# Graph attention, one core: the scaled accumulator enters TensorE's sum, and ScalarE writes it back

## The reference

```
q, k, v = x Wq + bq (scaled), x Wk + bk, x Wv + bv      # per node
s = sum over d of q[src] * k[dst]                        # per edge and head
attn = softmax of s over the edges with the same src
out[src] = sum of attn * v[dst];  y = layernorm(x + out Wo + bo)
```

## Time and profile before

| | us |
|---|---|
| three runs, median (lowest to highest) | 4021.01 (4016.24 to 4050.6) |
| the profiled execution: its time, its span | 4017.71, 4015.6 |
| busy: VectorE / GpSimd / TensorE / ScalarE | 3211.0 / 2447.6 / 2227.2 / 1504.6 |
| L931 gathers, 1794 of 1038 ns | 1863.0 busy, 583.7 idle before them |
| L790 and L797, 598 each, 952 and 946 ns | 569.2 and 565.5 |
| L844 and L836, 598 each, 429 and 426 ns | 256.6 and 255.0 |
| L1032 and L1034, 2392 and 1196 records | 902.0 and 497.3 |
| mean granted clock of TensorE | 0.743 of full speed |

### The profile page before, as it was taken

One profiled execution on the slowest core, in us unless ns is written; L12 is line 12 of the kernel. 1 busy time (PEld: TensorE's weight loads), 2 busy tenths in 40 slices (PEclk: granted clock), 3 DMA queues, 4 the chain that ended last, 5 costly groups with the idle time before them and its releaser, 6 DMA issues. The chain is left out here.

```text
span 4015.6 us, 59591 instructions
## 1 busy us (share of the span) xinstructions
PE 2227.2 (55%) x7109; PEld 1514.8 (38%) x7109; DVE 3211.0 (80%) x8164; ACT 1504.6 (37%) x6480; POOL 2447.6 (61%) x2365
## 2 busy tenths in 40 slices
PE   3999888653002555555555545555555555544776
PEld 3788775432001333333333333333333333323443
DVE  8554467799223999999999999999999999977776
ACT  0110002221001555555555555555555555534332
POOL 3221120003767777777777777777777777765677
PEclk9966568776555788778777787777877778766777
DMA  1211013226513788878887887888777788799222
GB/s 33 64 58 32 16 43 101 89 67 125 171 36 96 231 233 232 232 232 232 231 232 232 232 232 231 232 232 231 232 232 231 232 232 232 229 177 169 80 92 85
DMA packets 329217, 665.86 MB, mean 166 GB/s; under 512 B 63462, under 2 KB 191750, under 8 KB 329016
## 3 DMA queue, kind: packets, MB, share of 16 engines
q0 software_dynamic: 160768, 518.27, 46.4%
q1 hardware_dynamic: 168392, 146.96, 12.7%
HBM read 599.35 MB, written 65.86 MB: 166 GB/s over the span
## 5 line engine op out<-in xcount | busy, mean ns | idle before, releaser
L931 POOL DMA_INDIRECT kv<-kv_rows,idx x1794 | 1863.0, 1038 | 583.7 <-issue 538.5
L1032 PE MATMUL sum_ps<-pv,ident 128*128 128x264 f32 x2392 | 902.0, 512 | 1299.3 <-DVE pv L825 1299.3
L1032 PEld LDWEIGHTS sum_ps<-pv,ident 128*128 128x128 f32 x2392 | 511.3, 237 | 1712.1 <-DVE pv L825 1393.1
L987 ACT ACTIVATE pv<-kv,s 128x33 f32<-128x33 f32 x4784 | 1084.4, 309 | 53.9 <-ACT s L977 27.3
L790 DVE TENSOR_TENSOR prod<-kv,q 128x768 f32<-128x768 f32 x598 | 569.2, 952 | 59.7 <-DMA kv<-kv_rows,idx 59.6
L797 DVE TENSOR_REDUCE s<-prod 128x24 f32<-128x768 f32 x598 | 565.5, 946 | 0.0
L977 ACT ACTIVATE s<-s 128x32 f32<-128x32 f32 x598 | 137.0, 229 | 1126.1 <-DVE s L818 1126.1
L1034 PE MATMUL sum_ps<-pv,ident 128*128 128x264 f32 x1196 | 497.3, 508 | 0.0
L507 PE MATMUL hist_ps<-hot_lo,hot_hi 125*98 125x128 bf16 x1600 | 372.1, 409 | 121.7 <-DVE hot_hi L174 121.7
L825 DVE TENSOR_TENSOR pv<-kv,s 128x528 f32<-128x528 f32 x598 | 417.4, 698 | 0.3 <-ACT s L977 0.3
L507 PEld LDWEIGHTS hist_ps<-hot_lo,hot_hi 125*98 125x98 bf16 x1600 | 370.3, 259 | 123.2 <-issue 68.7
(11 more groups left out here) (164 smaller groups left out, 2450.5 us busy)
## 6 DMA issues: line engine op xcount, KB each, us to landing
q<-q_perm SPq DMA_DIRECT2D x598, 128.0 KB, 3.7
kv<-kv_rows,idx POOLq DMA_INDIRECT x1794, 4.0
kv_rows<-kv_st SPq DMA_DIRECT2D x98, 260.0 KB, 3.0
xt_sb<-in_xT SPq DMA_DIRECT2D x98, 128.0 KB, 3.2
node_rows<-q_st SPq DMA_DIRECT2D x98, 128.0 KB, 3.4
q_perm<-kv_st SPq DMA_DIRECT2D x98, 128.0 KB, 1.9
kv_st<-node_rows,node_id POOLq DMA_INDIRECT x98, 3.1
cols<-edge_keys,run_at POOLq DMA_INDIRECT x98, 2.5
```

The source lines that it names most:

```text
L931: pool.indirect_dma_start(out=kv[:, j, g, :], out_offset=None, in_=kv_rows, in_offset=bass.IndirectOffsetOnAxis(ap=idx[:, j, g:g + 1], axi ...
L987: last = act.activation(pv[:, b, V * VW + at_h:V * VW + at_h + HD + 1], kv[:, j, V, D + at_h:D + at_h + HD + 1], ACT.Copy, scale=s[:, b, V ...
L1032: pe.matmul(sum_ps[b][:, 0:VW], ident[:, :], pv[:, b, g * VW:(g + 1) * VW], start=g == 0, stop=False)
```

## The change

VectorE no longer adds the PSUM sum to the accumulator. It scales the accumulator of the step's tile into a fourth slot of `pv` (`carry`) and leaves `acc` as it is. TensorE takes that slot as a fourth product into the same bank, last. ScalarE then copies the finished bank into `acc` (`store`), with a table look-up of its own, in the middle of the next step's weighing: after three of the eight heads (BEFORE_STORE = 3). VectorE's `step` looks up first, now into two register sets rather than three, copies the old maximum right after the sum of products and before the weighing, and puts the carry between mask and maximum. ScalarE's copy of the indices moves from before the exponential to behind the weighing. The bound on the PSUM bank's reuse is now given by the order itself, so TensorE's wait for `acc_added` is gone, and its peeled steps with it. The table's scratch space moves from `pv` and `prod` into `kv`; `pv` grows by a slot.

```diff
@@ one_round @@
-        pv = sb("pv", [P, 2, G * VW])
-
-        room = pv[:, :, :].rearrange("p b w -> p (b w)")
...
+        pv = sb("pv", [P, 2, (G + 1) * VW])
+
+        room = kv[:, :, :, :].rearrange("p u g w -> p (u g w)")
...
@@ -797,9 +798,12 @@
                     dve.tensor_reduce(s[:, b, 0:G * HEADS], prod[:, :, :].rearrange("p g (h d) -> p (g h) d", d=HD),
                                       AX.X, ALU.add).then_inc(scored, 1)
 
-                def mask_scores(k, b, col, tile):
+                def old_maximum(k, b, tile):
 
                     dve.tensor_copy(s[:, b, G * HEADS:], runmax[:, bass.ds(tile * HEADS, HEADS)]).then_inc(old_copied, 1)
+
+                def mask_scores(k, b, col):
+
                     dve.wait_ge(scored, k + 1)
                     sv = s[:, b, 0:G * HEADS].rearrange("p (g h) -> p g h", h=HEADS)
                     dve.tensor_tensor(sv, sv, mflat[:, bass.ds(col, G)].unsqueeze(2).to_broadcast([P, G, HEADS]), ALU.add).then_inc(masked, 1)
@@ -827,50 +831,37 @@
                                       s[:, b, 0:V * HEADS].rearrange("p (g h) -> p g h", h=HEADS).unsqueeze(3).to_broadcast([P, V, HEADS, HD + 1]),
                                       ALU.mult).then_inc(pv_made, 1)
 
-                def scale_acc(k, b, tile, first=False):
-
+                def carry(k, b, tile, first=False):
                     if not first:
-                        dve.wait_ge(acc_added, k)
-                    dve.wait_ge(exp_made, k + 1)
-                    at_tile = acc[:, bass.ds(tile * VW, VW)].rearrange("p (h w) -> p h w", w=HD + 1)
-                    dve.tensor_tensor(at_tile, at_tile,
-                                      s[:, b, G * HEADS:].unsqueeze(2).to_broadcast([P, HEADS, HD + 1]), ALU.mult).then_inc(acc_scaled, 1)
-
-                def add_sum(k, b, tile):
-
-                    dve.wait_ge(acc_scaled, k + 1)
-                    dve.wait_ge(summed, k + 1)
-                    at_tile = acc[:, bass.ds(tile * VW, VW)]
-                    dve.tensor_tensor(at_tile, at_tile, sum_ps[b][:, 0:VW], ALU.add).then_inc(acc_added, 1)
+                        dve.wait_ge(acc_stored, k)
+                    dve.tensor_tensor(pv[:, b, G * VW:].rearrange("p (h w) -> p h w", w=HD + 1),
+                                      acc[:, bass.ds(tile * VW, VW)].rearrange("p (h w) -> p h w", w=HD + 1),
+                                      s[:, b, G * HEADS:].unsqueeze(2).to_broadcast([P, HEADS, HD + 1]), ALU.mult).then_inc(carry_made, 1)
 
                 dve.wait_ge(tab_ready, 1)
                 dve.wait_ge(runs_ready, 1)
 
-                tile_r = [dve.alloc_register(f"tile_{b}") for b in range(3)]
-                col_r = [dve.alloc_register(f"col_{b}") for b in range(3)]
-
-                def look_up(k, c):
+                tile_r = [dve.alloc_register(f"tile_{b}") for b in range(2)]
+                col_r = [dve.alloc_register(f"col_{b}") for b in range(2)]
+
+                def look_up(k, b):
                     v = dve.value_load(step_tab[0:1, bass.ds(k, 1)], min_val=0, max_val=TAB * C * P - 1)
-                    dve.reg_mov(tile_r[c], v & (P - 1))
-                    dve.reg_mov(col_r[c], v >> PBITS)
+                    dve.reg_mov(tile_r[b], v & (P - 1))
+                    dve.reg_mov(col_r[b], v >> PBITS)
 
                 def step(k, j, turn, peel=False, last=False):
 
                     b, b1 = j % 2, (j + 1) % 2
+                    tile, tile1, col1 = bounded(dve, tile_r[b], TILES), bounded(dve, tile_r[b1], TILES), bounded(dve, col_r[b1], TAB * C - G)
+                    look_up(k + 2, b)
                     score_sum(k + 1, b1, peeled=peel and j == 0)
+                    old_maximum(k + 1, b1, tile1)
                     weigh(k, j % U, b, peeled=peel and j < 2)
-
-                    tile, tile1, col1 = (bounded(dve, tile_r[j % 3], TILES), bounded(dve, tile_r[(j + 1) % 3], TILES),
-                                         bounded(dve, col_r[(j + 1) % 3], TAB * C - G))
-                    before = None if peel and j == 0 else bounded(dve, tile_r[(j + 2) % 3], TILES)
-                    look_up(k + 2, (j + 2) % 3)
-                    mask_scores(k + 1, b1, col1, tile1)
+                    mask_scores(k + 1, b1, col1)
+                    carry(k, b, tile, first=peel and j == 0)
                     maxima(k + 1, b1, tile1)
-                    if before is not None:
-                        add_sum(k - 1, b1, before)
                     if not last:
                         score(k + 2, (j + 2) % U, turn + (j + 2) // U)
-                    scale_acc(k, b, tile, first=peel and j == 0)
                     differences(k + 1, b1, tile1)
 
                 look_up(0, 0)
@@ -878,7 +869,8 @@
                 score(0, 0, 0)
                 score_sum(0, 0, peeled=True)
                 tile, col = bounded(dve, tile_r[0], TILES), bounded(dve, col_r[0], TAB * C - G)
-                mask_scores(0, 0, col, tile)
+                old_maximum(0, 0, tile)
+                mask_scores(0, 0, col)
                 maxima(0, 0, tile)
                 score(1, 1, 0)
                 differences(0, 0, tile)
@@ -891,10 +883,7 @@
                     step(k, k - LOOPS * B, LOOPS * (B // U), last=k == STEPS - 2)
                 k = STEPS - 1
                 weigh(k, k % U, k % 2)
-                tile, before = bounded(dve, tile_r[k % 3], TILES), bounded(dve, tile_r[(k - 1) % 3], TILES)
-                add_sum(k - 1, (k - 1) % 2, before)
-                scale_acc(k, k % 2, tile)
-                add_sum(k, k % 2, tile)
+                carry(k, k % 2, bounded(dve, tile_r[k % 2], TILES))
                 for r in tile_r + col_r:
                     dve.free_register(r)
 
@@ -976,39 +965,54 @@
                     act.wait_ge(diffs_made, k + 1)
                     act.activation(s[:, b, :], s[:, b, :], ACT.Exp).then_inc(exp_made, 1)
 
-                def weigh_last(k, j, turn, b, peeled=False):
+                def weigh_heads(j, b, heads):
+
+                    for h in heads:
+                        at_h = h * (HD + 1)
+                        last = act.activation(pv[:, b, V * VW + at_h:V * VW + at_h + HD + 1], kv[:, j, V, D + at_h:D + at_h + HD + 1],
+                                              ACT.Copy, scale=s[:, b, V * HEADS + h:V * HEADS + h + 1])
+                    return last
+
+                def weigh_last(k, j, turn, b, stored=True, peeled=False):
 
                     act.wait_ge(exp_made, k + 1)
                     act.wait_ge(kv_in[j], 16 * G * turn + 16 * G)
                     if not peeled:
                         act.wait_ge(summed, k - 1)
-                    for h in range(HEADS):
-                        at_h = h * (HD + 1)
-                        last = act.activation(pv[:, b, V * VW + at_h:V * VW + at_h + HD + 1], kv[:, j, V, D + at_h:D + at_h + HD + 1],
-                                              ACT.Copy, scale=s[:, b, V * HEADS + h:V * HEADS + h + 1])
-                    last.then_inc(last_made, 1)
+                    weigh_heads(j, b, range(0, BEFORE_STORE))
+                    if stored:
+                        store(k - 1, 1 - b)
+                    weigh_heads(j, b, range(BEFORE_STORE, HEADS)).then_inc(last_made, 1)
+
+                def store(k, b):
+
+                    v = act.value_load(step_tab[0:1, bass.ds(k, 1)], min_val=0, max_val=TAB * C * P - 1)
+                    tile = bounded(act, v & (P - 1), TILES)
+                    act.wait_ge(summed, k + 1)
+                    act.activation(acc[:, bass.ds(tile * VW, VW)], sum_ps[b][:, 0:VW], ACT.Copy).then_inc(acc_stored, 1)
 
                 act.wait_ge(tab_ready, 1)
                 act.wait_ge(runs_ready, 1)
                 for j in range(U):
                     indices(j, j, 0)
                 weights(0, 0)
-                weigh_last(0, 0, 0, 0, peeled=True)
+                weigh_last(0, 0, 0, 0, stored=False, peeled=True)
                 for k in range(B):
-                    indices(k + U, k % U, 1)
                     weights(k + 1, (k + 1) % 2)
                     weigh_last(k + 1, (k + 1) % U, (k + 1) // U, (k + 1) % 2, peeled=k == 0)
+                    indices(k + U, k % U, 1)
                 with act.Fori(1, LOOPS - 1) as kk:
                     for j in range(B):
                         k = kk * B + j
-                        indices(k + U, j % U, kk * (B // U) + j // U + 1)
                         weights(k + 1, (j + 1) % 2)
                         weigh_last(k + 1, (j + 1) % U, kk * (B // U) + (j + 1) // U, (j + 1) % 2)
+                        indices(k + U, j % U, kk * (B // U) + j // U + 1)
                 for k in range((LOOPS - 1) * B, STEPS - 1):
+                    weights(k + 1, (k + 1) % 2)
+                    weigh_last(k + 1, (k + 1) % U, (k + 1) // U, (k + 1) % 2)
                     if k + U < STEPS:
                         indices(k + U, k % U, (k + U) // U)
-                    weights(k + 1, (k + 1) % 2)
```

(29 more changed lines are left out.)

## The result

| | before | after |
|---|---|---|
| median (lowest to highest) of four runs each, us | 4022.43 (4016.24 to 4050.6) | 4185.89 (4173.09 to 4188.99) |
| the profiled execution: its time, its span | 4017.71, 4015.6 | 4187.79, 4185.8 |
| mean granted clock of TensorE | 0.743 | 0.770 |

The ratio is 1.0386, with a 95% interval of 1.0333 to 1.0440: the change makes the kernel slower, by 163 us. The forecast was 4030, no change; rival B had 4180.

A forecast was written before the change was run, and what follows sets the result against it. VectorE bounds the kernel now at 4.01 us a step; afterwards GpSimd's gathers, partly held, would give 4.02. 556 steps x 0.01 = +6 us, 4017.7 + 6 + 3.3 = 4027, say 4030 us; own range 3985 to 4060, with rivals 3955 to 4200.

The forecast's parts named there:

- rival B: Third gather held by VectorE's product every second step: 4.3 us a step, 4180 us; chance 0.31 together with D.
- VectorE's own step: VectorE alone, after removed work and the moved look-up: about 3.7 us a step instead of 3.98, bounds 3.2 to 3.9.
- The look-up ahead of the reduction: Table look-up's register work on VectorE, moved before the sum of products: gives back 0.5 us a step.
- ScalarE's copy back: One more copy out of PSUM per step, 0.38 us; ScalarE's chain 2.65 us of 3.9, room enough.
- TensorE's longer chain at the slow clock: Fourth product delays sum, copy and next carry at 1.2 GHz: 4.05 us a step, taken for 45% of the time.
- GpSimd takes over: VectorE's average 3.86 us falls below the gathers' 3.90, so the product starts when its gather lands.
- the count of collisions: How often a third gather starts inside VectorE's product: one in half of the six-step spells, 4.02 us a step.
- My spell of six steps: Three fast-clock and three slow-clock steps: 3.93 us a step without a collision, 4.10 with one.
- The price of one: A third gather held by the product ends 0.8 us late; that step takes 4.89 us.
- Rival A: GpSimd sets the pace without collisions: 3.93 us a step, 3976 us, 3960 at the floor; chance 0.27.
- C: GpSimd does not bind, its gaps between gathers shrink; VectorE at 3.7 us at both clocks, 3855 us; chance 0.06.
- D: Indices a step later leave fewer gathers in flight in the tail: +44 us on any case; chance counted within B's 0.31.

The follow-up runs named there:

- e11: e5 with GpSimd gathering only two of three slots after the first six steps, so the layer is not computed: 3708.9 us.
- e3: The kernel before without VectorE's addition of the PSUM sum and the waits for it, so the result is not the layer's: 4191.61 us.
- e9: Control for e4: ScalarE copies q into PSUM and the product waits for it, but reads q from SBUF: 4162.73 us.
- e4: The changed kernel with ScalarE copying q into PSUM each step and VectorE's product reading q from there: 4054.54 us.
- e5: e4 with the exponentials also written to PSUM, from which VectorE's weighing and carry read their factors: 3944.39 us.
- e7: The changed kernel with ScalarE's copy of the indices back at its old place before the exponential: 4180.84 us.
- e10: The kernel before with ScalarE copying q into PSUM and VectorE's product reading q from there: 4011.05 us.

## Why the prediction was right and wrong

- **VectorE's own step, taken as 3.7 us.** Right: 3.59 in e11. The look-up ahead of the reduction was taken as 0.5 us a step; it shows as 0.36 there and 0.27 in after.
- **ScalarE's copy back, hidden.** Right: 391 ns against 383 from the earlier trace rows, and VectorE waits 23 us for it in 437 steps.
- **TensorE's longer chain at the slow clock, 4.05 us a step.** It did not bind: the carry's whole idle time is 26 us, 0.06 a step, and the gathers' 4.35 is longer. The fourth product is not in e3, which is as slow. The 4.05 itself is not shown by any run.
- **GpSimd takes over.** Right, with the sign named beforehand: the product's idle time went from 0.0 to 318 us, released by the DMA, and the gaps stayed 0.30.
- **The step that failed is the count of collisions**: "At the slow clock VectorE is the slower one (4.05), GpSimd gets ahead and is safe", and behind it "I take half of each". That let one third gather in twelve be held and made 4.02 us. 263 of 437 were, and 196 second ones by the weighing and the carry, which the forecast left out. The slow clock protects nothing: of the 179 products that start while 1.2 GHz is granted 101 hold a third gather, of the 258 that start at 2.4 GHz 162. VectorE waits for the landing in both spells (383 of 437 products), so the landing places its product. Where the product holds the next step's third gather it starts 2.77 us (median) after the end of its own step's third gather, where it holds none 3.12 us. My own landing times, 2.5 to 3.06 us against 2.91, already put the third gather inside the product most of the time. My spell of six steps began each time with VectorE behind; it is ahead in nearly every step.
- **The price of one.** Too high: I took 0.8 to 1.0 us for a held third gather; the mean is 0.52 (0.31 x 437 / 263). More and cheaper ones, and 0.12 a step from the weighing and the carry, made nearly the sum of rival B, 4.3 us a step and 4180 us; measured 4.35 and 4186. That the sum agrees so closely is partly luck. B had a chance of 0.31. B's mechanism and place are shown (e9 against e4: 108 us by one operand); its rule "every second step" fits only roughly (263 of 437).
- **Rival A and C.** A's floor of 3960 is about what e5 reaches (3944), once the holds are taken away by other means. C is excluded: 0.305 is the gap in every kernel with three gathers a step.
- **D, indices a step later.** Not seen: e7 undoes it and stays at 4181, and the last 37 steps took 3 us more, where D had 44.
- **What I read into the kernel before.** I counted its held gather as a cost of 0.07 us that ties the engines together. The tie is there, the cost is not: VectorE never waits for it, and e10 gains nothing to speak of. It is the first gather of a step that is held, in each of the 474 steps, by 0.10 us on average. That is what a spare of 0.1 us on GpSimd's side looks like, and the same spare disappears when VectorE gets faster.

The rule itself came from single rows and held: 529 of 552 gathers. The Trainium skill (SBUF — State Buffer, Who interferes with whom) says that a VectorE instruction with at most one SBUF input, outside the modes that use two ports, does not contend with GpSimd; the traces of e5 agree, with 482 overlaps at 998 ns. Its inference in the same section that a tensor_tensor with two SBUF inputs does not hold descriptor work is contradicted by the trace of every kernel here whose product or weighing has two (after: 263 third gathers held by the product). The mask and the differences, 0.18 us each, keep two in e5 and are too short to tell.

## What to carry to other kernels

When two engines share something and are within a few per cent of each other, a cut on the busier one may only change who waits for whom: before cutting, look where the waits will put the starts, not only how much work is left. A filler that makes a kernel faster is a quick test for that. If a GpSimd that issues gathers is the bound, look first for VectorE instructions with both inputs in SBUF at the gathers' starts, and move one input to PSUM: here that turned a loss of 163 us into a gain of 72 to 78 (3950 and 3944 against 4022; 2.0 and 2.6% on their own chips).

## What the runs showed of the hardware

- An indirect gather of 128 rows cost GpSimd 0.998 us and a gap of 0.305: 3.908 us for three, which e5 keeps to over 500 steps (390.8 us per hundred).
- A held gather ends 0.87 us after the end of the VectorE instruction that holds it, so holding costs nearly its whole remaining length. One that started 0.03 us ahead of the product was not held, and the product was not longer for it (0.96 us). The 34 products of after that start within 0.05 us of a gather's start took 970 ns on average, the 162 that start further into one 957.
- Reading the broadcast operand from PSUM made the big instructions no slower: product 950 ns against 961, weighing 696 against 703.
